# Order of the first loads of an attention stage: context ahead of latents and of the key and value weights

## The reference, cut to what matters

```python
def rms_norm(x, w): return x * rsqrt(mean(x * x, -1) + 1e-6) * w

lat = layernorm(x)                                # (4, 256, 512)
kv  = concatenate([context, lat], axis=1)         # (4, 1857, 512)
q   = rms_norm(heads(lat @ Wq), q_norm_w)         # 32 heads of 128
k   = rms_norm(heads(kv @ Wk), k_norm_w)          # 8 heads, each for 4 query heads
v   = heads(kv @ Wv)
out = softmax(q @ k.T / sqrt(128)) @ v
x   = x + tanh(g_xattn) * (join(out) @ Wo)

xf    = layernorm(x)
inter = xf @ c1_w.T @ c2_w.T
idx   = argmax of each block of 32 of the 1792 values of inter
h     = relu(w1[idx] . xf)
x     = x + tanh(g_ffn) * (h @ w2t[idx])
```

## Time and profile before

| | us |
|---|---|
| median of 3 runs | 3189.39 |
| lowest and highest | 3186.25, 3190.24 |
| the profiled execution's own time | 3180.85 |
| its span in the trace | 3178.9 |

### The profile page before, as it was taken

The page is one execution under the profiler, slowest core; times in us unless marked ns, Lnnn a source line. Parts: engine busy times, 40 slices in busy tenths (PEclk is TensorE's granted clock), DMA queues, the critical chain, the costliest instruction groups (busy, mean ns, idle before and its releaser), DMA issues. The chain is left out here.

```text
span 3178.9 us, 51790 instructions
## 1 busy us (share of the span) xinstructions
PE 2994.5 (94%) x14650; PEld 2438.6 (77%) x14650; DVE 2464.9 (78%) x3317; ACT 2048.6 (64%) x2899; POOL 1325.0 (42%) x791
## 2 busy tenths in 40 slices
PE   7996999999899999998999999999999997797899
PEld 6874888888678888886788888778888885585677
DVE  7773888888958888887788888868888888413765
ACT  3443787787858778876787777767787786311211
POOL 2330455555525555554355555535555555000000
PEclk9997999999999999999999999999999998898899
DMA  7873010011211110112111110210011000734200
GB/s 261 276 217 109 31 40 33 33 49 34 75 35 40 40 33 33 36 34 86 34 34 43 34 39 33 74 50 32 33 41 41 33 27 11 227 97 138 89 30 20
DMA packets 183908, 210.87 MB, mean 66 GB/s; under 512 B 10965, under 2 KB 125653, under 8 KB 182761
## 3 DMA queue, kind: packets, MB, share of 16 engines
q1 hardware_dynamic: 179016, 196.27, 19.2%
q0 software_dynamic: 2176, 8.39, 0.8%
q10 hardware_dynamic: 2592, 4.72, 0.5%
HBM read 140.14 MB, written 69.21 MB: 66 GB/s over the span
## 5 line engine op out<-in xcount | busy, mean ns | idle before, releaser
L878 POOL TENSOR_TENSOR att_sm<-att_sm,att_sc 128x1024 f32<-128x1024 f32 (+1 forms) x384 | 853.8, 2223 | 672.2 <-DVE att_pr L829 671.7
L684 PE MATMUL att_ppv<-att_pr,att_V 128*128 128x512 f32 (+1 forms) x2880 | 847.9, 404 | 25.2 <-DVE att_pr L829 22.8
L664 PE MATMUL att_pqk<-att_q,att_kT 128*128 128x512 f32 (+1 forms) x2880 | 849.9, 404 | 6.6 <-issue 3.4
L756 ACT ACTIVATE att_sc<-att_pqk,att_rk 128x512 f32<-128x512 f32 (+1 forms) x960 | 659.9, 688 | 184.2 <-PE att_pqk L664 182.3
L625 PE MATMUL att_pkv<-att_ctxT,att_wkv 128*128 128x512 f32 (+1 forms) x3072 | 758.8, 377 | 2.4 <-issue 1.2
L829 DVE TENSOR_TENSOR att_pr<-att_sc,att_pr 128x1024 fp32r<-128x1024 f32 (+1 forms) x512 | 645.1, 1261 | 37.5 <-ACT att_pr L767 37.5
L625 PEld LDWEIGHTS att_pkv<-att_ctxT,att_wkv 128*128 128x128 f32 x3072 | 561.6, 190 | 122.1 <-issue 2.1
L684 PEld LDWEIGHTS att_ppv<-att_pr,att_V 128*128 128x128 f32 (+1 forms) x2880 | 532.5, 191 | 152.5 <-DVE att_pr L829 38.8
L664 PEld LDWEIGHTS att_pqk<-att_q,att_kT 128*128 128x128 f32 (+1 forms) x2880 | 505.8, 185 | 122.0 <-ACT att_sc L756 14.4
L823 DVE TENSOR_TENSOR att_sc<-att_sc,att_pmax 128x1024 f32<-128x1024 f32 (+1 forms) x512 | 585.4, 1143 | 16.4 <-PE att_pmax L633 16.2
L767 ACT CAST att_pr<-att_sc 128x1024 fp32r<-128x1024 f32 (+1 forms) x512 | 510.3, 997 | 112.4 <-PE att_ppv L684 110.9
(11 more groups left out here) (131 smaller groups left out, 2679.8 us busy)
## 6 DMA issues: line engine op xcount, KB each, us to landing
q_scr<-pre_qT SPq DMA_DIRECT2D x128, 256.0 KB, 3.6
att_wkv<-kv_scr SPq DMA_DIRECT2D x64, 512.0 KB, 3.9
att_q<-q_scr SPq DMA_DIRECT2D x64, 512.0 KB, 4.3
o_scr<-att_on SPq DMA_DIRECT2D x64, 256.0 KB, 2.0
out_oraw<-o_scr SPq DMA_DIRECT2D x64, 256.0 KB, 4.8
att_sc<-in_ctx SPq DMA_DIRECT2D x16, 768.0 KB, 4.9
pre_wq_raw<-in_L_xattn_Wq SPq DMA_DIRECT2D x8, 1024.0 KB, 6.7
kv_scr<-pre_kv SPq DMA_DIRECT2D x8, 1024.0 KB, 7.5
```

What stands on the lines that cost most here:

```text
L664: mm = pe.matmul(pqk[0:m, (h * NT + t) % 2], kT[:, kp, t * P:t * P + m], q[:, qp, h], start=(i == 0), stop=(i == 2))
L684: mm = pe.matmul(ppv[:], V[0:m, vp, t], pr[0:m, pp, (t // 2) % NP, t % 2], start=(t == 0 and i == 0), stop=(t == NT - 1 and i == 2))
L756: act.activation(sc[0:m, h, t], pqk[0:m, s % 2], ACT.Copy, scale=rk[0:m, t:t + 1]).then_inc(sc_ok, 1)
L878: pool.tensor_tensor(sm[0:m, 0:w], sm[0:m, 0:w], sc[0:m, h, i:i + w], ALU.add).then_inc(sum_ok, w)
```

## The change

Only the window `START` is touched. Its loads get places of their own: 21 is added to the latents' place, 41 to that of the keys' weights, 30 to that of the values' weights, and nothing to the four of the context. Before, the places in `START` (after the shift by -60) were -58 for the keys' weights, -40.4 for the values', -40.3 for the latents and -34.5 to -24.5 for the context. Now they are -34.5 to -24.5 for the context, -19.3 for the latents, -17 for the keys' weights and -10.4 for the values'. The list `loads` itself, from which the other windows are made, stays as it was. The load of the first queries stays behind all of them.

```diff
         start_early = [x for x in early if x[1] not in ("ldwk", "ldwv")]
-        START = window((0, -2 * UT, loads), (0, 0, context), (0, UT - 3.33, start_early))
+        first = dict(ldlat=21, ldwk=41, ldwv=30, ldx=0)
+        first_loads = [(p + first[what], what, h, t) for p, what, h, t in loads]
+        START = window((0, -2 * UT, first_loads), (0, 0, context), (0, UT - 3.33, start_early))
```

## The result

The changed kernel takes 3178.53 us, the median of 7 runs (3173.33 to 3180.78), the kernel before beside it 3188.19 us, the median of 7 runs (3183.6 to 3191.69). The ratio is 0.9972, 95% interval 0.9961 to 0.9982: 9 us less, between 5.7 and 12.4. The forecast was 3183.6 us, in a range of 3178.0 to 3189.5, from a shift of 5.8 us. The time lies near the low end. The ratio of this measurement is on the side of faster, for which 0.39 had been given, but its interval reaches across the bound of 0.998. Two more measurements of the same kernel gave 0.9988 (0.9979 to 0.9997) and 0.9979 (0.9970 to 0.9988). The mean of the three is 0.9980, 6.5 us of 3188.

What follows compares the result with a forecast made beforehand. The opening of attention was taken as bound by x0's transfer, the rest as one chain of work. A 5.8 us shift with zero for the clock, applied to the median of 3189.39, gave 3183.6 us, range 3178.0 to 3189.5.

Steps and rivals of the forecast that it cites:

- shift of 5.8 us: Opening of attention: x0 at the queue's head moves the first transpose from 260.99 to 255.2 us; bounds 5.5 and 6.0.
- What bounds the opening: Head of the attention stage: bound by one transfer, x0, with TensorE 23.03 us without work before its first transpose.
- the middle of the rows, 4.8: x0's assumed landing time in us, from three later-batch loads without load ahead: 4.6, 4.8 and 5.1 us.
- The supply of the other tiles: Transposes: x1, x2 and x3 land before their tiles want them, the tightest with 1.6 us to spare; cost nothing.
- Latents and weights at the back: Queue behind the context: latents land at 264.8, keys' weights at 266.2, values' at 267.6 us; cost nothing.
- The room of 4.5 us: Keys' weights landing at 266.2 us would be 4.5 us ahead of the first key chunk at 270.7.
- the fit to x0: Landing formula for the opening's loads: last byte at 375 GB/s after 254 us, plus 1.06 us to be seen.
- The first key chunk near 270.7 us: After the transposes: the chunk starts at 270.7 instead of 276.50 us, released by VectorE.
- The clock, zero, with ends of -3.3 and +7.1: TensorE's clock in the opening: unknown sign, taken as zero; 3.3 us better or 7.1 us worse possible.
- The sign of being wrong: Clock row of the opening: stretches of 0.50 lying on other chunks than before would show the forecast wrong.
- the clock falls better: Rival, chance 0.12: both half-clock key chunks run at full speed, -3.3 us more, giving 3180.3 us.
- Same or faster: Whole kernel: same 0.57, faster 0.39, slower 0.04; the bound for faster is 3183.0 us, the forecast 3183.6.

Runs made afterwards that it cites:

- the five executions of the table: Profiled executions without edits: the kernel before twice, openings 43.93 and 42.61 us, and the changed kernel three times, openings 33.71, 37.56 and 33.68 us.

## Why the prediction was right, point by point

- *What bounds the opening.* Right: TensorE waited for x0 alone, and its landing sets the first transpose, 4.5 to 4.7 us behind the first load in three executions.
- *The shift of 5.8 us, 5.5 to 6.0.* Right, a little small, since x0 took 4.6, 4.4 and 4.6 us where the middle of the rows, 4.8, had been taken: 10.67 and 10.84 became 4.48 to 4.65 (6.0 to 6.4), or 5.8 to 6.2 from TensorE's last start in the first stage. It could be called right from a trace because this distance repeats, while the part from the first scores to the end spreads by 7 us over the five executions of the table. The mean of three ratios gives 6.5 us. The distance of the profiled execution before from the medians, left unexplained in the sum, goes with the clock: 3180 us and 0.976 for 3187 and 0.973.
- *The supply of the other tiles.* Right: in the first profile x1 landed 6.8 us behind the first load for the 7.1 worked out, and no tile waited for a DMA.
- *Latents and weights at the back.* Right in that they cost nothing, too sure in its size. The room of 4.5 us was 1.74, 4.5 and 1.9 us in the three profiles of the changed kernel, and 1.05 MB more used it up in one execution. Two things were left out: a load far back in a full queue is mostly seen about 1 us later than the fit to x0 says, and a clock that rises early shortens the work that hides the loads. The latents landed 15.7, 14.2 and 14.4 us behind the first load for the 14.5 worked out.
- *The first key chunk near 270.7 us.* It began at 270.39 us, but that is partly luck: SP's first load came 1.3 us later than assumed, and the faster clock of the transposes gave back 1.4. Counted from the first load it is 18.8, 19.9 and 18.8 us for 20.4. The first scores stood 8.9, 4.4 and 9.5 us earlier than in the profile before, not 5.8.
- *The clock, zero, with ends of -3.3 and +7.1.* The sign was rightly left open. The sign of being wrong that was named for it, half-clock stretches on other chunks than before, did appear: zero doesn't describe a single execution. The first profile had a clock better by 4.2 us in the opening, more than the end of -3.3, since the transposes had been left out of that end; the next execution had it at half for most of the transposes again. The kernel before moved its stretches too, so at least a part of this is chance; that none of it is an effect of the order isn't shown. The rival "the clock falls better" gave the picture of two profiles of three, but not the kernel's mean.
- *Same or faster.* The forecast put the likeliest time 0.6 us on the side of no change. The first measurement, 0.9972, was on the other side, and the three together stand on the bound itself. The shift would have had to be sized to within 10% to tell. That the first time fell inside the range, 0.5 us above its low end, rests on the width given to the runs' spread as much as on the shift.
- *The Trainium skill, "DMA: Bandwidth & Descriptors", on the anatomy of one DMA*, would have had x0 land after 3.8 us, an estimate from its figures. It gives them for transfers issued by GpSimd, and these are issued by SP. The traces show 4.6, 4.4 and 4.6 us in the three executions. *The Trainium skill, "TensorE: Matmul & The Clock Gate"*, on the clock gate, says that the moment of the rise differs between runs. The executions above agree, from before 261 us to about 268 for one kernel.

## What to carry to other kernels

At the opening of a stage, put in the queue first what the first step of the chain needs, and price the move by the bytes that leave its front: here 1 MB was 3.2 to 3.6 us, where the rate of 375 GB/s seen in the trace gives 2.8. Work out the room of what moves to the back with the fast version of the work that hides it, and look at the issuing engine too: the issue of eight loads held SP for 8 us, and a barrier behind them held TensorE too. Where TensorE's clock rises and falls in the stretch, compare distances between fixed points in several executions and don't credit one profile's clock to the change.

## What the hardware showed that was not expected

One kernel's executions differ in the opening by up to 3.9 us (33.68 to 37.56) through the place of the half-clock stretches alone, and in one execution 18 transposes of the identity ahead of the real ones didn't raise the clock: it was at 0.50 for 15.5 us with TensorE busy for 12.67 of them, as the window of that kernel has it:

```profile
251.50:267.00 15.50, 12.67 (x54) 10.13 (x54) 5.54 (x8) 4.69 (x8) 0.00 (x0) 0.50 0.97 329
```

SP's issue of a load isn't of a fixed length: the two weight loads took 0.84 us at the head of the queue and 4.36 us behind the five of the context and the latents. With the weights back at the head and the latents behind the context, it was the queries' two loads behind them that took 6.91 us.
